# Second attention: score keys in four column tiles, and score chunks moved between the halves of the weighted product

## The reference, cut to what matters

```python
x = conv_attention(x)                      # first attention, on 4 x 256 x 32 x 32
t = to_tokens(x)                           # 4 batches of 1024 tokens, 256 wide
u = layer_norm(t)
q, k, v = split_heads(u @ w_qkv)           # 8 heads of 32
attn = softmax(q @ k.T * 256 ** -0.5)      # 1024 queries x 1024 keys, a head
t = t + merge_heads(attn @ v) @ w_out + b_out
t = t + mixture_of_experts(layer_norm(t))  # 8 experts, 2 for each token
```

## Time and profile before

| what | value |
|---|---|
| time, median of 3 runs | 1183.72 us (1182.17 to 1184.16) |
| span of the profiled execution, first to last instruction | 1183.2 us |
| PE busy | 1105.0 us, 93% of the span, 10344 matmuls |
| weight loads on PE | 728.7 us, 62% |
| DVE busy | 818.8 us, 69% |
| ACT busy | 628.7 us, 53% |
| POOL busy | 600.2 us, 51% |
| mean granted TensorE clock | 0.985 of full speed |

### The profile page before, as it was taken

The page is one execution under the profiler, slowest core; times in us unless marked ns, Lnnn a source line. Parts: engine busy times, 40 slices in busy tenths (PEclk is TensorE's granted clock), DMA queues, the critical chain, the costliest instruction groups (busy, mean ns, idle before and its releaser), DMA issues.

```text
span 1183.2 us, 28483 instructions
## 1 busy us (share of the span) xinstructions
PE 1105.0 (93%) x10344; PEld 728.7 (62%) x10344; DVE 818.8 (69%) x1493; ACT 628.7 (53%) x1144; POOL 600.2 (51%) x513
## 2 busy tenths in 40 slices
PE   7999999978999999999999989898999999999995
PEld 4454645434444454555445545687899988989883
DVE  4666566766788788788878892768555656655773
ACT  3566676546677666766775665453333333333332
POOL 3424242314888763775477546167545445544540
PEclk9999999989999999999999999999999999999999
DMA  5356842626123230433243213723333233323328
GB/s 173 89 181 211 311 160 94 184 69 196 51 56 87 82 82 29 104 100 98 68 115 91 60 43 100 303 38 77 53 54 54 43 52 55 46 46 47 46 38 289
DMA packets 98884, 120.60 MB, mean 102 GB/s; under 512 B 29024, under 2 KB 76064, under 8 KB 98112
## 3 DMA queue, kind: packets, MB, share of 16 engines
q1 hardware_dynamic: 75280, 70.40, 20.3%
q0 software_dynamic: 20400, 42.08, 15.9%
q10 hardware_dynamic: 3072, 6.30, 1.5%
HBM read 73.10 MB, written 45.47 MB: 100 GB/s over the span
## 4 chain that ended last, share of the span: by engine, by line
PE 70%; DVE 11%; issue 6%; DMA 6%; ACT 3%; DVEq 3%; POOL 1%; SPq 1%; ACTq 0%; POOLq 0%
PE PP L1023 21%; PE PP L1448 11%; PE PP L1307 9%; PE PP L1333 8%; PE PP L1122 3%; DVE mxp L1739 3%; PE PP L1254 3%; PE PP L1194 3%; PE PP L1039 3%; PE PP L1322 2%; PE PP L1317 2%; DMA res_d<-WORK,lb 2%; PE PP L1154 1%; DVEq L2016 1%; DVE WORK L2017 1%
## 5 line engine op out<-in xcount | busy, mean ns | idle before, releaser
L953 ACT ACTIVATE WB<-PP 128x512 f32<-128x512 f32 x512 | 268.6, 606 | 146.1 <-PE PP L1333 146.0
L1739 DVE TENSOR_REDUCE mxp<-PP 128x2 f32<-128x1024 f32 x242 | 287.0, 1219 | 62.3 <-PE PP L1254 62.0
L993 ACT ACTIVATE WORK<-PP,b1c 128x256 f32<-128x256 f32 (+1 forms) x320 | 139.4, 450 | 239.4 <-PE PP L1023 191.7
L699 POOL TENSOR_TENSOR WB<-WB 128x1024 f32<-128x1024 f32 x84 | 197.8, 2358 | 89.4 <-PE PP L1322 58.7
L782 POOL DMA_INDIRECT res_d<-WORK,lb x70 | 117.6, 1680 | 157.8 <-DVE WORK L2034 144.7
L1448 PE MATMUL PP<-WB,WORK 128*128 x1704 | 193.8, 274 | 0.0
L1023 PE MATMUL PP<-WORK,WB 128*128 128x256 f16 (+1 forms) x1552 | 175.9, 273 | 2.4 <-DVE WORK L2003 1.7
L1448 PEld LDWEIGHTS PP<-WB,WORK 128*128 128x128 f16 x1704 | 165.2, 98 | 19.6
L1023 PE MATMUL PP<-WORK 128*128 128x128 f16 (+6 forms) x1086 | 161.1, 300 | 11.3 <-DVE WORK L1656 3.6
L1023 PEld LDWEIGHTS PP<-WORK,WB 128*128 (+1 forms) x1552 | 152.2, 102 | 22.2 <-issue 4.8
L1333 PE MATMUL PP<-WORK 97*128 97x256 f16 x1024 | 158.0, 277 | 6.7 <-ACT WB L953 4.2
(11 more groups left out here) (319 smaller groups left out, 1205.1 us busy)
## 6 DMA issues: line engine op xcount, KB each, us to landing
WORK<-in_L_ffn_W_dram POOLq DMA_DIRECT2D x32, 512.0 KB, 4.3
res_d<-WORK SPq DMA_DIRECT2D x8, 1024.0 KB, 5.2
late_d<-WB POOLq DMA_DIRECT2D x1, 6144.0 KB, 19.3
WB<-late_d ACTq DMA_DIRECT2D x3, 2048.0 KB, 14.0
v_d<-WORK SPq DMA_DIRECT2D x4, 1024.0 KB, 5.2
WORK<-q_hi_d SPq DMA_DIRECT2D x16, 256.0 KB, 3.7
WORK<-v_d SPq DMA_DIRECT2D x8, 512.0 KB, 5.6
WORK<-k_hi_d SPq DMA_DIRECT2D x16, 256.0 KB, 3.9
```

Source lines behind the costliest of these rows:

```text
L699: pool.tensor_tensor(PS[n % 2], PR[n % 3][:, 0], PR[n % 3][:, 1], ALU.add).then_inc(s("pair_kept"), 1)
L953: act.activation(PR[n % 3][:, c // 2, c % 2 * 2:c % 2 * 2 + 2], SCORES[m % 3] .rearrange("p (h n) -> p h n", h=2), ACT.Exp).then_inc(s("e_ ...
L993: act.activation(hid[:, k, 0:width], hidden_bank(k)[:, 0:width], ACT.Gelu, bias=b1c[:, bass.ds(e, 1), k], scale=1.0 / WSCALE)\
L1739: dve.tensor_reduce(mxp[:, n // 4 % 2, i, h:h + 2, k], PP[2 + h // 2][:, :].rearrange("p (h n) -> p h n", h=2), X_AXIS, ALU.max).then_inc( ...
```

## The change

A score matmul of 97 x 128 becomes four of 97 x 32: the 128 keys of a block are cut in four, and each quarter goes to its own column tile and its own 32 partitions of the same bank. There are 32 score matmuls and 32 loads in a step where there were 8 and 8. In the step, `weigh_heads` is cut into its two halves, and the order becomes: chunks 0 and 1, the maxima group, the first half of the weighed product (with its two waits), chunk 2, the second half, chunk 3, the sums, then the full-width piece if there is one. ACT's, DVE's, POOL's and SP's programs are unchanged.

```diff
-            def weigh_heads(n):
+            def weigh_heads(n, i):
                 par, s4 = n // 16 % 2, n % 4
-                pe.wait_ge(s("e_kept"), 4 * n + 4)
-                if s4 == 0:
-                    pe.wait_ge(s("sum_kept"), FREE + n // 4)
-                for i in range(2):
-                    for h in range(GH):
-                        pe.matmul(WEIGHED[h * D:(h + 1) * D, 0:QN], VV[par][:, 2 * s4 + i, h * D:(h + 1) * D],
-                                  PR[n % 3][:, i, h], start=(s4 + i == 0), stop=(s4 + i == 4),
-                                  skip_group_check=True)
+                if i == 0:
+                    pe.wait_ge(s("e_kept"), 4 * n + 4)
+                    if s4 == 0:
+                        pe.wait_ge(s("sum_kept"), FREE + n // 4)
+                for h in range(GH):
+                    pe.matmul(WEIGHED[h * D:(h + 1) * D, 0:QN], VV[par][:, 2 * s4 + i, h * D:(h + 1) * D],
+                              PR[n % 3][:, i, h], start=(s4 + i == 0), stop=(s4 + i == 4),
+                              skip_group_check=True)
...
-                    mm = pe.matmul(SCORES[m % 3][:, i * QN:(i + 1) * QN], KP[g][0:QK_ROWS + 1, h, j * P:(j + 1) * P],
-                                   QP[0:QK_ROWS + 1, g, h, q:q + QN], start=(i == 0), stop=True,
-                                   skip_group_check=True)
+                    for r in range(P // D):
+                        keys = slice(j * P + r * D, j * P + (r + 1) * D)
+                        mm = pe.matmul(SCORES[m % 3][r * D:(r + 1) * D, i * QN:(i + 1) * QN],
+                                       KP[g][0:QK_ROWS + 1, h, keys], QP[0:QK_ROWS + 1, g, h, q:q + QN],
+                                       start=(i == 0), stop=True, skip_group_check=True)
...
-                    for c in range(3):
-                        if n == 0 and c == 2:
-                            pe.wait_ge(s("mx_kept"), 2 * MAX_EARLY)
+                    for c in range(2):
                         score_chunk(n, c)
...
-                    for m in groups[0:1]:
+                    for m in groups:
                         max_group(m, b, before)
+                    if n >= LAG:
+                        weigh_heads(n - LAG, 0)
+                    if n == 0:
+                        pe.wait_ge(s("mx_kept"), 2 * MAX_EARLY)
+                    score_chunk(n, 2)
+                    if n >= LAG:
+                        weigh_heads(n - LAG, 1)
                     score_chunk(n, 3)
                     if n >= LAG:
-                        weigh_heads(n - LAG)
                         sum_heads(n - LAG)
-                    for m in groups[1:2]:
-                        max_group(m, b, before)
...
             for n in range(B * STEPS - LAG, B * STEPS):
-                weigh_heads(n)
+                weigh_heads(n, 0)
+                weigh_heads(n, 1)
                 sum_heads(n)
```

## The result

| | changed | before, same chip | ratio, 95% interval |
|---|---|---|---|
| first comparison | 1192.35 us (4 runs) | 1183.94 (4) | 1.0062 [1.0041, 1.0083] |
| second comparison | 1193.24 us (6) | 1183.89 (17) | 1.0074 [1.0045, 1.0104] |

The changed kernel is slower by 8.4 us in the first and 9.4 us in the second comparison (from 4.9 to 9.8 and from 5.3 to 12.3 by the intervals). The forecast was +4.8, with 1181 to 1198 as the range.

The account below looks back on a forecast made before the run. PE was taken to bound the second attention, with DVE's loop holding plain steps at 2.86 us. Terms 1.6 - 0.5 + 7.5 - 0.6 - 1.0 - 0.3 + 0.3 - 2.2 = +4.8 us gave 1188.5; range 1181 to 1198.

Parts of the forecast that it names:

- 9 projection steps with the copy: Second attention, three per batch: waiting for ACT's copy adds 0.64 us each; the five others per batch gain 0.11 in length.
- waiting steps of the first batch: Six steps with t % 4 = 2, where ACT copies the sums: 3.01 to 3.28 us, +0.27 each, +1.6.
- plain steps: Steps without a full-width piece: DVE's loop holds them at 2.86 us, -0.04 each, -0.5 for 12.
- direct steps: Steps with four groups of sums, PE's loop over DVE's: 3.33 to some 3.05 us, -0.27 each.
- low clock at t = 20: Rival: idler PE lets the granted clock fall to 1.2 GHz, +1.6 us per place, possibly +10 or more; chance 0.05.
- last group to last product: Last seven steps, without maxima groups: chunk 3 no longer waits 0.31 us for ACT, fewer form changes; together -2.2 us.
- steps 12 to 20: Each of three batches: two savings and one milder wait (+0.3), the rest DVE's; -0.2 a batch, -0.6 us.
- The copy's wait: Steps with t % 4 = 2: first half product waits for ACT's copied sums, starting about 1.73 us behind score start.
- slow tiles: Rival: score tiles miss the pace; +9 us at 0.125 us a group, +95 at 0.216; chance 0.2, mostly small end.
- the start of a matmul: Rival: starting a load and matmul pair takes 62 ns, PE's plain step 3.7 us, about 1300 us; chance 0.02.
- The rival in which they overlap: Maxima group's form changes cost less than 0.10 us: -6.4 us at zero, some -10 side by side; chance 0.18.
- the rival named for step 18 in the mixed order: Experiment's rival: POOL's later adds fall on other DVE instructions and take the gain back, within 1 us; no chance given.

Follow-up runs that it names:

- second comparison: The changed kernel run again with no edit, beside the kernel before on one chip: 1193.24 us, ratio 1.0074.
- the kernel before, second profile: The kernel before, unedited and profiled again: 1183.97 us, span 1182.1.
- copy first: ACT's copy of the sums moved ahead of the exponential of chunk 0, on the changed kernel: 1173.76 us, 0.9921 of the kernel before.
- tiles alone: The kernel before with scores in four column tiles, old order kept: 1179.43 us, ratio 0.9971.
- copy first on the kernel before or on tiles alone: ACT's copy ahead of the exponential: on the kernel before 1178.83 us against 1182.27 (0.998); on column tiles in the old order 1173.79 us (0.9926).
- order alone: The changed kernel with wide score matmuls, so the new order without tiles: 1237.32 us, 1.0452 of the kernel before.
- mixed order: Column tiles and ACT's copy moved ahead, new order only in the last seven steps: 1172.04 and 1172.38 us, 0.9915 and 0.9916 of the kernel before.
- step 18 direct: Step 18 added to the direct steps (eight sum products, no POOL pair add): on tiles, moved copy and late new order 1166.02 us; on the changed kernel 1180.48.

## Why the prediction was right, and where its sizes were off

The direction and the mechanism were right. The sum was 4.8 us. From the start of the first score to the start of the last product the stage grew from 452.95 us (the kernel before, second profile) to 460.13 and 458.39, so by 7.2 and 5.4, and the timed difference was 8.4 and 9.4. The time lies inside the range, but above the 1186.5 to 1191 that the prediction called likeliest. Term by term, distances of both profiles of the changed kernel less those of the kernel before:

| term | forecast | profile 1, 2 |
|---|---|---|
| 9 projection steps with the copy | +5.8 | +6.05, +6.04 |
| 15 projection steps | +1.7 | +1.8, +1.8 |
| waiting steps of the first batch | +1.6 | +2.1, +1.9 |
| waiting steps among direct ones, t = 18, 22, 26 | +2.4 | +2.6, +2.6 |
| plain steps | -0.5 | -0.9, -0.9 |
| direct steps | -4.0 | -3.0, -2.7 |
| t = 13 and 19, three batches | 0 | +1.5, +1.5 |
| low clock at t = 20 | rival | +2.2, +2.4 |
| one group of the last batch, t = 23 | 0 | -1.7, -1.7 |
| row steps, t = 30, change of batch, first four steps | 0 | +0.1, -2.0 |
| last group to last product | -2.2 | -3.5, -3.5 |
| sum | +4.8 | +7.2, +5.4 |

(The forecast's terms stand here by kind of step: its -0.6 for steps 12 to 20 is 3 x 0.3 of waiting and -1.5 of direct steps, and its -1.0, -0.3 and +0.3 behind them are split in the same way. In the second batch two distances, t = 25 to 27, are up to 0.9 us longer in the profiles of the changed kernel, at differing steps; -3.0 and -2.7 hold some of it, the rest is with the row steps.)

- **The copy's wait.** Forecast 1.73 us from scores to first half, measured 1.74; forecast +0.27, +0.64 and +0.31 for the three kinds of waiting step, measured +0.31, +0.69 and +0.355. Each is 0.04 to 0.05 over, by which the wait was undersized, some 0.7 us in the three rows of waiting steps. The three at t = 30 that the prediction left out grew by 0.31 to 0.36 too, but the changes of batch behind them took it back. With the copy first none of the 28 is left in the trace.
- **Tiles keep the pace.** Yes, 0.22 us a chunk and no more. The rivals of slow tiles and of the start of a matmul are out. The Trainium skill, "TensorE: Matmul & The Clock Gate", section "Weight-path perf modes", says that a 32-column load loses the fast weight load; nothing of it is seen, a tile's load lasts 97 ns in the median and a wide one's 98.
- **The two changes around the group** cost about 0.10 each, as priced (group to product 316.16 - 315.84 = 0.32 with the copy first, where its 512 columns take 0.22). The rival in which they overlap is out: a direct step came to 3.07, where the forecast was 3.05.
- **Plain step.** 2.86, DVE's bound, as said. No plain step of any run here is shorter.
- **Projection.** +0.12 for +0.11.
- **The tail was larger than -2.2**, but by something else. Before, in both profiles, group 23 of the last batch waited 1.47 and 1.46 us for DVE, and then the low clock made products and sums behind it longer. From PE's timeline of the kernel before, second profile:

```profile
708.72 0.39 PE L1254 MATMUL PP<-WB 32*128 32x512 f16 x4 [1.46 <-DVE mxp L1739]
709.05 0.39 PE L1333 MATMUL PP<-WORK 97*128 97x256 f16 x2
709.37 1.78 PE L1307 MATMUL PP<-WB,WORK 128*32 128x256 f32 x16
710.91 1.95 PE L1317 MATMUL PP<-WB,onesf 128*32 128x256 f32 x16
```

  1.78 and 1.95 us for what takes some 1.07 each at full clock. The changed kernel has neither: 1.7 us at t = 23 and 1.3 us behind the last group, beyond the -2.2 forecast, given back that no step of the prediction held.
- **What the prediction left out** on the other side is t = 19 (+0.31 each) and t = 13 (+0.17 to +0.19), DVE held by POOL, +1.5.
- **The clock** was priced as a rival at +1.6 a place, with a chance of 0.05. It fell, at t = 20, behind PE's wait at t = 19. The stage of the changed kernel, as the earlier trace rows, and one such fall, as the earlier trace rows:

```profile
289.00:751.00 462.00, 418.56 (x8193) 248.48 (x8195) 351.15 (x550) 325.14 (x585) 298.63 (x258) 0.98 0.30 80
705.50:709.72 4.22, 4.22 (x61) 2.20 (x58) 2.82 (x5) 1.72 (x4) 0.00 (x0) 0.60 0.11 32
```

  The three batches with this place saw it in two each time in the changed kernel (second and fourth; second and third), once and never in the kernel before, three times with copy first and with tiles alone, and never with copy first on the kernel before or on tiles alone, nor with the order alone, nor in the four profiles with the mixed order or step 18 direct. Every profile with a fall there has the long wait at t = 19, but five with that wait have no fall. It is 2.2 to 2.4 us of the loss, at a mean granted clock of 0.60, that is at 1.2 GHz for most of the stretch. What decides it is not the change alone, since the kernel before did both; **it stays open.**

So the step that failed is the term for the steps t = 12 to 20: -0.6 was forecast, and the distances show +3.1 and +3.4, lost to DVE's hold and the clock. The end of the stage gave 3.0 us back that were no more foreseen. The two nearly cancel, and that the sum came so near is luck to that extent. That the time is longer by 8.4 and 9.4 us and the stage by 5.4 and 7.2 is within the intervals, and stages that the change doesn't touch vary by as much: the same instructions ahead of the first score took from 287.2 to 291.9 us over these profiled executions, those from the start of the last product on 436.0 to 443.3. The two ends of the first range, 287.2 and 291.9, are the mixed order and the changed kernel; no run ties that to the change (the mixed order's repeat had 291.7), and it wasn't traced further.

## What to carry to other kernels

When work is moved forward in one engine's order, look up where its producer stands in the *other* engine's order: here two lines in ACT's program were worth 15 to 16 us of the stage and 19.5 us of the time, more than the change had lost. A change of tile form costs about 0.1 us each time, so what a tile form is worth is the number of changes it saves, and only in steps where PE is last; where DVE or its read of a projection is, the same order can lose. Price from one meeting point of the two engines to the next, and look there too for small instructions of a shared resource that the new timing puts side by side.

## What was not expected: a small DVE instruction held by POOL

At t = 19 DVE turns 128 x 16 numbers to integers (CAST). From the timelines of DVE and POOL, in the changed kernel (second profile):

```profile
466.15 2.33 DVE L1870 CAST idx<-rs 128x16 int32<-128x16 f32 x1
```

```profile
466.07 2.37 POOL L699 TENSOR_TENSOR WB<-WB 128x1024 f32<-128x1024 f32 x1 [10.69 <-PE PP L1317]
```

in the kernel before (second profile):

```profile
463.06 1.72 DVE L1865 CAST idx<-rs 128x16 int32<-128x16 f32 x1
```

```profile
462.40 2.36 POOL L699 TENSOR_TENSOR WB<-WB 128x1024 f32<-128x1024 f32 x1 [10.55 <-PE PP L1317]
```

and with step 18 direct in the mixed order, where POOL's long add isn't there at this time:

```profile
L1874 DVE CAST idx<-rs x4: 174/174/176, 457.5 to 752.5; 128x16 int32<-128x16 f32 x4
```

The CAST takes 0.174 us when it is alone, so also with the order alone, where POOL's adds fall elsewhere and the distance at t = 19 is 3.66 us. Otherwise it ends when POOL's add ends, whenever it began: 468.48 and 468.44, 464.78 and 464.76. It holds DVE's next reduction and with it the next group, so the group distance at t = 19 is 4.86 us before, 5.18 after the change (POOL's add now starts beside the CAST and not 0.66 us ahead of it), and 3.05 with step 18 direct.

From the mixed order to that, t = 19 is 1.8 us shorter in each of three batches, 5.3 us together, while the stage is 5.3 us shorter than in the repeat of the mixed order and 3.7 than in its first profile. The losses are at t = 17 (below) and t = 20 (0.25 each in two batches); the rest varies. On the changed kernel t = 19 is shorter by 1.65, 1.7 and 2.1, 5.5 of the 9.2 and 7.4 us by which its stage is shorter than in the two profiles without; 1.7 and 2.0 more come at t = 20 (the clock), and the rest lies at places that vary. The hold also moved: POOL's next add now falls beside another small instruction of DVE at t = 17, a TENSOR_TENSOR that there lasts 0.56 to 0.74 instead of 0.17 us and ends within 0.02 us of the add; in two of three batches that distance is 0.4 to 0.6 us longer. So the rival named for step 18 in the mixed order came true in part.

The Trainium skill, "SBUF — State Buffer", section "SBUF: two separate sides", says that some DVE operations share a pair of ports with POOL as an exclusive lock for the whole of an instruction. The rows of CAST and add agree, to 0.04 us. The same is seen in a smaller TENSOR_SCALAR at t = 13 (0.17 us before, 0.33 to 0.34 in the changed kernel). The one whose 1.83 us made group 23 late in the kernel before also ends with an add, 0.04 us behind it, but it had begun 0.63 us ahead of the add, beside one of POOL's DMA_INDIRECT; so what held it at first is not the add. That it is the port, and not something else that DVE and POOL share, was only argued: no run put the CAST's operands elsewhere.
